# Attention and expert FFN on one core: the work behind the last head in a new order, three shared gates in banks y0, y1 and o, and the product for a pair's common tokens in high and low halves

## What is computed

```python
x = x + layernorm(attention(layernorm(x)))      # x: 8 x 512 x 256, 16 query heads, 4 key/value heads, D = 128, causal
x = x + layernorm(ffn(layernorm(x)))
# ffn, over the 4096 tokens:
scores = softmax(x @ gate_w.T)                  # 64 experts
topk_w, topk_idx = top_k(scores, 6)
# each expert takes the first CAP = 64 of the tokens that chose it:
d = (silu(buf @ w_gate) * (buf @ w_up)) @ w_down            # F = 176
y = sum of topk_w * d over a token's experts
y = y + (silu(x @ sh_gate.T) * (x @ sh_up.T)) @ sh_down.T   # shared expert, F_SH = 352
```

## Time and profile before

| what | us |
|---|---|
| median of 3 runs (1421.34 to 1427.04) | 1422.0 |
| the profiled execution | 1422.52 |
| its span in the trace | 1420.7 |
| the last output projection ends, the stage behind the heads begins | 1199.1 |
| first gather issued | 1241.56 |
| last scatter issued | 1374.23 |

### The profile page before, as it was taken

How to read it: one execution, slowest core, us unless ns; L and a number is a source line. 1 busy time by engine, 2 the same in 40 slices (tenths; PEclk the granted TensorE clock), 3 DMA queues, 4 the chain that set the end, 5 groups by cost and what they waited for, 6 DMA issues and landing times.

```text
span 1420.7 us, 27053 instructions
## 1 busy us (share of the span) xinstructions
PE 1331.6 (94%) x8963; PEld 1183.5 (83%) x8963; DVE 1098.7 (77%) x3655; ACT 843.2 (59%) x2315; POOL 799.9 (56%) x1052
## 2 busy tenths in 40 slices
PE   4999999999999999999999999999999998898950
PEld 3899999999999999999999999999999997854530
DVE  6777786889778977888788868896889788643438
ACT  5666666666666666666666666666666665443424
POOL 3666565556555655556455655565656554556644
PEclk9999999999999999999999999999999999898985
DMA  8100000100010001000100001000100017889986
GB/s 301 50 1 1 16 16 9 34 24 16 2 42 24 16 2 42 23 1 16 43 23 1 16 9 42 16 16 7 36 23 16 1 35 215 223 244 276 304 263 272
DMA packets 50235, 96.50 MB, mean 68 GB/s; under 512 B 4689, under 2 KB 36914, under 8 KB 50098
## 3 DMA queue, kind: packets, MB, share of 16 engines
q1 hardware_dynamic: 43954, 85.33, 18.5%
q0 software_dynamic: 6144, 9.44, 3.2%
HBM read 68.27 MB, written 26.49 MB: 67 GB/s over the span
## 4 chain that ended last, share of the span: by engine, by line
PE 86%; DVE 6%; POOL 3%; issue 2%; DMA 2%; ACT 1%; DVEq 0%; POOLq 0%; ACTq 0%
PE bank_s L623 19%; PE bank_t L623 19%; PE bank_o L623 17%; PE bank_y L623 12%; PE bank_f L623 8%; PE bank_t L708 4%; PE bank_s L708 4%; PE bank_f L708 2%; DMA ffn_sums<-dsum,idx_s 2%; POOL ffn_sums L1889 1%; DVE fstat L1679 1%; DVE fa L1674 1%; POOL xg L1876 1%; DVE fa L1699 1%; DVE pt_l L1352 0%
## 5 line engine op out<-in xcount | busy, mean ns | idle before, releaser
L1747 POOL TENSOR_TENSOR prob<-prob,rinv 128x512 f32<-128x512 f32 (+3 forms) x512 | 368.7, 726 | 320.8 <-DVE rinv L1346 309.9
L983 ACT ACTIVATE prob<-prob,negmax 128x512 f32<-128x512 f32 (+3 forms) x512 | 285.3, 557 | 85.1 <-DVE negmax L1333 76.8
L1734 POOL TENSOR_TENSOR q_l<-q_sum,q_h 128x128 fp32r<-128x128 f32 x254 | 182.5, 740 | 25.2 <-ACT q_h L963 25.2
L623 PE MATMUL bank_o<-pt_h,v_h 128*128 128x128 f32 (+3 forms) x512 | 180.0, 352 | 1.3 <-DVE pt_l L1352 1.3
L623 PE MATMUL bank_o<-pt_l,v_h 128*128 128x128 f32 (+3 forms) x512 | 165.1, 323 | 0.0
L623 PE MATMUL bank_o<-pt_h,v_l 128*128 128x128 f32 (+3 forms) x512 | 165.1, 322 | 0.0
L623 PE MATMUL bank_y<-wo_h,o_h 128*128 128x256 f32 x512 | 143.7, 281 | 3.2 <-DVE o_l L1358 2.8
L623 PE MATMUL bank_y<-wo_h,o_l 128*128 128x256 f32 x512 | 143.6, 280 | 0.0
L623 PE MATMUL bank_y<-wo_l,o_h 128*128 128x256 f32 x512 | 143.1, 279 | 0.0
L999 ACT ACTIVATE o_h<-bank_o,bkv_s 128x512 fp32r<-128x512 f32 x128 | 88.2, 689 | 78.1 <-PE bank_o L623 77.9
L992 ACT ACTIVATE pt_h<-bank_t 128x512 fp32r<-128x512 f32 (+3 forms) x208 | 89.1, 429 | 53.1 <-PE bank_o L623 50.9
(11 more groups left out here) (425 smaller groups left out, 4118.7 us busy)
## 6 DMA issues: line engine op xcount, KB each, us to landing
w_gu<-in_w_in SPq DMA_DIRECT2D x32, 704.0 KB
w_dn<-in_w_out SPq DMA_DIRECT2D x32, 320.0 KB
xio<-in_x SPq DMA_DIRECT2D x16, 512.0 KB, 4.3
token_table<-rows SPq DMA_DIRECT2D x8, 640.0 KB, 3.7
ffn_sums<-keys SPq DMA_DIRECT2D x4, 1024.0 KB
x_rows<-xio SPq DMA_DIRECT2D x8, 512.0 KB, 2.9
ffn_sums<-ytr SPq DMA_DIRECT2D x16, 256.0 KB, 2.1
fx<-x_rows SPq DMA_DIRECT2D x8, 512.0 KB
```

Source lines behind the costliest of these rows:

```text
L623: return pe.matmul(o, l, r, start=start, stop=stop, skip_group_check=True)
L983: act.activation(p_, p_, ACT.Exp, bias=negmax[:, r, i:i + 1], scale=-1.0, accum_out=rsum[:, r, i:i + 1]).then_inc(exp_made, 1)
L1734: pool.tensor_tensor(l_[:, cols], sum_of(step)[:, cols], plain(h_)[:, cols], ALU.subtract).then_inc(pos_low, 1)
L1747: pool.tensor_tensor(p_, p_, rinv[:, r, i:i + 1].to_broadcast([P, (i + 1) * P]), ALU.mult).then_inc(prob_made, 1)
```

## The change

Behind the heads:

- `LEFT`: three gate steps, (L1, 0, 0), (L1, 0, 1) and (LAST, 1, 0), use the banks y0, y1 and o instead of ring banks.
- `GATES`: the two steps that DVE does are now n = 2 of batch L1 (96 columns); n = 0 of it go over ACT and POOL.
- PE begins with four gates, puts halves of two gates between the transposes and the router products, turns each mask half at once, and makes `shared_down(L1, 1)` right behind. Each engine's order is written anew to fit.
- `shift` (a 128 x 4 product) moves from DVE to POOL; the softmax weights move from DVE to ACT (four activations with a scale), in one piece after one reciprocal; the second half's logits have a buffer of their own.
- POOL makes the first gate product between the two pairs of inverse roots, and begins the second only when DVE has finished the norm (`x2_normed`).
- SP stores the token rows before the weights of pairs 10 and 11; pair 11's are loaded behind `firsts_dram`.
- POOL's gathers wait for `gather_made`, which DVE sets behind the two casts to `idx_g`, not for `index_made`, three small instructions later.

In the experts' stage `add_second` has two float32r passes (`sec_h`, `sec_l`) for one float32 product: ACT makes `sec_h` with one more copy, DVE makes `sec_l` with one more subtraction (`second_rest`), which stands behind `half_w` of the pair after next.

```diff
-        GATES = ((L1, 1, 1), (L1, 1, 2), (L1, 0, 1), (L1, 0, 2), (LAST, 1, 0), (LAST, 1, 1), (LAST, 1, 2),
+        GATES = ((L1, 1, 0), (L1, 1, 1), (L1, 0, 0), (L1, 0, 1), (LAST, 1, 0), (LAST, 1, 1), (LAST, 1, 2),
                  (LAST, 0, 0), (LAST, 0, 1), (LAST, 0, 2))
+        LEFT = {step: Chan(bank[n], sem(f"{n}_gate_full"), sem(f"{n}_gate_taken"))
+                for step, n in ((("gu", L1, 0, 0), "y0"), (("gu", L1, 0, 1), "y1"), (("gu", LAST, 1, 0), "o"))}
...
-            for j in range(NWA, NW):
+            for j in range(NWA, NW - 2):
                 load_pair(j)
             store_rows(LAST)
-            store_ffn(LAST - 1, 1)
+            load_pair(NW - 2)
+            store_ffn(L1, 1)
             store_x2(LAST)
...
+            load_pair(NW - 1)
             sp.wait_ge(dma_firsts, 16)
...
             for n in range(NF):
-                gate_up(LAST - 1, 1, n)
-            gate_up(LAST - 1, 0, 0)
-
-            for step in (turn_x2, route):
-                for k in range(2):
-                    step(LAST, k)
-            gate_up(LAST - 1, 0, 1)
-            gate_up(LAST - 1, 0, 2)
-
+                gate_up(L1, 1, n)
+            gate_up(L1, 0, 2)
+
+            pe.wait_ge(var_made, VARS.index(("x2", LAST, 0)) + 1)
+            gate_up(L1, 0, 0, (0,))
+            turn_x2(LAST, 0)
+            gate_up(L1, 0, 0, (1,))
+            turn_x2(LAST, 1)
+            route(LAST, 0)
+            pe.wait_ge(var_made, VARS.index(("x2", LAST, 1)) + 1)
+            gate_up(L1, 0, 1, (0,))
+            route(LAST, 1)
+            gate_up(L1, 0, 1, (1,))
             turn_mask(LAST, 0)
-            gate_up(LAST, 1, 0, (0,))
+            gate_up(LAST, 1, 0)
             turn_mask(LAST, 1)
-            gate_up(LAST, 1, 0, (1,))
+
+            shared_down(L1, 1)
             gate_up(LAST, 1, 1)
-            shared_down(LAST - 1, 1)
             gate_up(LAST, 1, 2)
-            shared_down(LAST - 1, 0)
...
             def add_second(j):
 
                 pe.wait_ge(same_made, j + 1)
-                pe.wait_ge(second_made, j + 1)
-                mm(bank[f"t{j % 2}"][0:CAP, 0:E], same[j % 2][CAP:2 * CAP, :], dsum[j % ND][CAP:2 * CAP, :], stop=True
-                   ).then_inc(same_in, 1)
+                pe.wait_ge(second_low, j + 1)
+                to, at_ = bank[f"t{j % 2}"][0:CAP, 0:E], slice(CAP, 2 * CAP)
+                mm(to, same[j % 2][at_, :], sec_h[at_, :])
+                mm(to, same[j % 2][at_, :], sec_l[at_, :], stop=True).then_inc(same_in, 1)
...
                 act.wait_ge(down_in, j + 1)
-                act.activation(dsum[j % ND][CAP:2 * CAP, :], bank[f"t{j % 2}"][CAP:2 * CAP, 0:E], ACT.Copy
-                               ).then_inc(second_made, 1)
+                d_ = bank[f"t{j % 2}"][CAP:2 * CAP, 0:E]
+                act.activation(sec_h[CAP:2 * CAP, :], d_, ACT.Copy)
+                act.activation(dsum[j % ND][CAP:2 * CAP, :], d_, ACT.Copy).then_inc(second_high, 1)
...
+            def second_rest(j):
+                at_ = slice(CAP, 2 * CAP)
+                dve.wait_ge(second_high, j + 1)
+                dve.tensor_tensor(sec_l[at_, :], bank[f"t{j % 2}"][at_, 0:E], plain(sec_h[at_, :]), ALU.subtract
+                                  ).then_inc(second_low, 1)
...
+            pool.wait_ge(x2_normed, LAST + 2)
             gate_product(1)
...
-            pool.wait_ge(index_made, 1)
+            pool.wait_ge(gather_made, 1)
```

More of the change, by code:

```diff
@@ L207, in build @@
         second = place("second", [P, 3, NP], F32)
-        same = [place(f"same{i}", [P, CAP], F32) for i in range(2)]
+        same = [place(f"same{i}", [P, CAP], F32R) for i in range(2)]
         twice = [place(f"twice{i}", [P, 1], F32) for i in range(2)]
@@ L374, in use, with logit_of @@
             return c.bank, c.full, c.taken, u
+        VARS = [("x", 0)]
+        for b_ in range(NB):
+            if b_:
+                VARS.extend([("y", b_ - 1), ("x2", b_ - 1)])
+            if b_ < LAST:
+                VARS.append(("x", b_ + 1))
+        VARS.extend([(name, LAST, k) for name in ("y", "x2") for k in range(2)])
+        def logit_of(b, k):
+            return logit_b if (b, k) == (LAST, 1) else logit
         def x2_of(b, k):
@@ L1025, in route @@
                     c = 2 * k + i
-                    last = act.activation(rows[:, c, E:ROW], logit[:, i, 0:NE], ACT.Exp, bias=rmax[:, c:c + 1],
+                    last = act.activation(rows[:, c, E:ROW], logit_of(b, k)[:, i, 0:NE], ACT.Exp, bias=rmax[:, c:c + 1],
                                           accum_out=psum_[:, c:c + 1])
@@ L1137, in gate_in_high @@
                 act.activation(lanes[lane][0][0:fn, n, :], made[0:fn, :], ACT.Copy).then_inc(a_high[lane], 1)
-            gate_tanh_(L1, 1, 0)
             gate_out(0)
             gate_out(1)
-            gate_tanh_(L1, 0, 0)
+            gate_tanh_(L1, 1, 2)
+            gate_in_high(0)
+            gate_tanh_(L1, 0, 2)
             turn_x2(LAST, 0)
-            gate_high(L1, 1, 0)
             turn_x2(LAST, 1)
-            gate_in_high(0)
-            gate_high(L1, 0, 0)
             gate_in_high(1)
+            gate_high(L1, 1, 2)
+            gate_out(2)
             route(LAST, 0)
-            gate_out(2)
+            gate_out(3)
             route(LAST, 1)
-            gate_out(3)
             gate_in_high(2)
+            gate_out(4)
+            gate_in_high(3)
+            gate_high(L1, 0, 2)
+            act.wait_ge(sums_inverted, 1)
+            for c in range(TT):
+                last = act.activation(rows[:, c, E:ROW], rows[:, c, E:ROW], ACT.Copy, scale=pinv[:, c:c + 1])
+            last.then_inc(weights_made, 2)
+            gate_out(5)
             act.wait_ge(shift_made, 1)
@@ L1168, in scalar_program @@
             gate_out(7)
+            shared_down(L1, 0)
             gate_in_high(6)
@@ L1248, in variance @@
                 last.then_inc(var_made, 1)
-            VARS = [("x", 0)]
-            for b_ in range(NB):
-                if b_:
-                    VARS.extend([("y", b_ - 1), ("x2", b_ - 1)])
-                if b_ < LAST:
-                    VARS.append(("x", b_ + 1))
-            VARS.extend([(name, LAST, k) for name in ("y", "x2") for k in range(2)])
             def normed(o, s_, i):
@@ L1389, in route @@
                 done(dve.tensor_copy(left[:, :, 0:NE], halves[:, :, 1, :]))
-                dve.tensor_tensor(logit[:, :, 0:NE], halves[:, :, 0, :], left[:, :, 0:NE], ALU.add).then_inc(taken, 1)
+                dve.tensor_tensor(logits[:, :, 0:NE], halves[:, :, 0, :], left[:, :, 0:NE], ALU.add).then_inc(taken, 1)
                 dve.wait_ge(taken, u + 1)
                 for i in range(2):
-                    last = dve.max(top8[:, i, :], logit[:, i, :])
+                    last = dve.max(top8[:, i, :], logits[:, i, :])
                 done(last)
@@ L1397, in route @@
                 for i in range(2):
-                    last = dve.match_replace(left[:, i, :], top8[:, i, :], logit[:, i, :], -BIG)
+                    last = dve.match_replace(left[:, i, :], top8[:, i, :], logits[:, i, :], -BIG)
                 done(last)
@@ L1583, in vector_program @@
                     step(LAST, k)
+            dve.wait_ge(router_exp, 2 * LAST + 2)
+            dve.reciprocal(pinv[:], psum_[:]).then_inc(sums_inverted, 1)
             for r in range(CAP // 8):
@@ L1619, in vector_program @@
                 at_ = slice(u * CAP, (u + 1) * CAP)
-                dve.tensor_copy(idx_g[at_, :], turned[at_, 0, :, u])
+                last = dve.tensor_copy(idx_g[at_, :], turned[at_, 0, :, u])
+            last.then_inc(gather_made, 1)
             dve.tensor_copy(idx_s[0:CAP, :], turned[0:CAP, 1, :, 0])
@@ L1649, in expert_act @@
                 last.then_inc(half_made, 1)
+                if j > 1:
+                    second_rest(j - 2)
                 dve.wait_ge(half_made, j + 1)
@@ L1670, in vector_program @@
                 targets(j)
+            second_rest(NP - 2)
+            second_rest(NP - 1)
             def add_sums(b):
```

74 lines of the change are left out of this document (43 added, 31 removed).

## The result

The changed kernel takes 1418.95 us (median of 15 runs, 1416.31 to 1420.56) against 1423.40 us for the kernel before in the same series (15 runs, 1421.34 to 1427.60). The ratio is 0.9971, with a 95% interval of 0.9960 to 0.9981: a gain of 4.5 us, 0.3%, less than the 0.5% that the prediction calls measurable. Forecast were 1412.3 us and a range up to 1418.5. The profiled execution took 1418.23 us with a span of 1416.4, against 1422.5 and 1420.7.

A forecast was written before the change was run, and what follows sets the result against it. Late POOL and PE, not the picks, were taken to bound the first gather, and DMA the experts' stage: 1422.5 - 10.5 (earlier gather) + 0.8 (gathers meeting loads) - 0.5 (cheaper add_second) = 1412.3 us, range 1406.5 to 1418.5.

The forecast's parts named there:

- picks at 1214.55 (1214.6): DVE behind the heads: shorter waits and moved work let the picks start at 1214.6, 4.1 us earlier.
- POOL done at 1229.74 (1229.3): POOL behind the heads: with waits for ACT cut to 2.0 us, done at 1229.3, 10.3 earlier.
- the forecast gain of 10.2: Whole kernel: from 1422.5 us to 1412.3 us.
- tables at 1228.4: DVE behind the picks: tables done at 1228.4, or 1230.5 if three small steps each wait for POOL.
- 0.3 for DVE steps beside POOL: Before the first gather: allowance of 0.3 us for small DVE steps waiting on POOL, giving 1231.0.
- 1228.5 as forecast: PE before the tables: its last shared_down product, waiting for POOL's low half, ends at 1228.5.
- I charge 0.8 for the first (0 to 3): First gather: meeting pair 11's weights and firsts in flight costs 0.8 us, from 0 to 3.
- - 0.5 (the halves): Experts' stage: of 7.8 us from the cheaper add_second on PE, only 0.5 counted, for the last rounds.
- the distance from first gather to last scatter of 132 us: Experts' stage: distance stays at 132 us; a change beyond 3 us either way means the prediction is wrong.
- that the whole gain reaches the end rests on this: Experts' stage: first weight reload follows the first pair's output, so the saturated DMA stretch begins 10 us earlier.
- part is given back: Rival: clock drop, ACT starving POOL, gathers colliding with pair 11, or scatter stalls leave 4 to 7 us, 1417; chance 0.24.
- Slower: Rival, experts' rounds: ACT's copy and DVE's subtraction delay add_second, losing 0.57 us a round, 1430; chance 0.04.

The follow-up runs named there:

- tables_alone: Changed kernel, but POOL starts its last gate product only when DVE's tables are done: 1415.82 us (one run).
- pair11_late: Changed kernel with pair 11's weights loaded behind the last two stores of the feed-forward sums, not ahead of the gathers: 1417.51 us, ratio 0.9930.
- light versions: Kernel before and changed kernel, both without the second expert's gate and up weights in pairs 12 to 31: 1411.49 us (0.9905) and 1404.63 us (0.9855).
- order_only: Changed kernel with the old float32 product for the common tokens, so only the new order behind the heads: 1417.89 us, ratio 0.9937.
- order_pair11: Changed kernel with the old float32 product and pair 11's weights loaded behind the last two stores of the sums: 1414.96 us, ratio 0.9929.
- series 3: Two by two on one chip: changed kernel with halves or float32 product, pair 11's weights ahead of gathers or behind the stores: 1415.92 to 1418.63 us.
- halves_only: Kernel before with only the common tokens' product changed, to high and low halves: 1426.98 us, ratio 1.0002.
- halves_but_last_p11: Changed kernel with the float32 product in the last six pairs and pair 11's weights behind the last stores: 1414.56 us, ratio 0.9920.
- best_float: Changed kernel with the float32 product for all pairs and pair 11's weights behind the last stores: 1416.89 us, ratio 0.9939.
- (light): Changed kernel with halves against the same with float32 product, both without some weight loads in pairs 12 to 31: 1402.02 against 1404.55 us.
- the first four series: The first four of five groups of follow-up runs, each version's ratio taken to the kernel before on the same chip.
- f_order: Changed kernel with the old float32 product, pair 11's weights still ahead of the gathers: 1417.36 us, ratio 0.9933.
- after_again: Changed kernel measured again, unchanged: 1419.86 us, ratio 0.9962.

## Why the prediction was wrong

Behind the heads the working held nearly to the letter: picks at 1214.55 (1214.6), the norm's second half at 0.73 instead of 1.52, no clock drop in front of the tables, POOL done at 1229.74 (1229.3). The error is in four terms, and they add up to the 5.9 us between the forecast gain of 10.2 and the 4.3 of the profiled executions.

- **"tables at 1228.4"**, with "0.3 for DVE steps beside POOL": 1230.26. I wrote down that the small steps could wait for POOL, with 2.1 us and an end at 1230.5, and put 0.3 into the sum. Four of the six steps took 0.6 to 0.8 us each, against 0.18 to 0.34 for all six in tables_alone. That agrees with the rule of the Trainium skill that the prediction cites, page SBUF — State Buffer, section "SBUF: two separate sides", that whoever starts first holds the shared ports for its whole instruction. PE's product in front of the tables ended at 1229.3 and not at 1228.5 as forecast, and PE then stood 0.99 us for the tables. The two delays together cost 1.6 us, 1.0 of it by the tables; 0.3 were in the sum, and 1.3 of 10.5 went: the first gather came at 1232.3 for 1231.0.
- **"I charge 0.8 for the first (0 to 3)"**: 1.8. The mechanism was right, only the size was off by 1.0. pair11_late, back at 8.2 us from gather to activation, shows that the load of pair 11 was all of it.
- **"- 0.5 (the halves)"**, and with it "the distance from first gather to last scatter of 132 us": the distance became 136.8, beyond the 3 us that I had named as the sign of an error. Of the 4.1 us more, 1.8 are the gather's landing, 0.3 net lie between the first activation and the last reload, and 2.1 behind the last reload. Of these 2.1 only the last pair's part is shown: with the new order and the float32 product the same stretch was 32.2 to 34.2 us in five profiles with all loads, against 32.3 before and 34.4 here. Shown is that the halves lengthen the last pair's chain by 1.1 to 2.2 us, which my sum did not contain: I priced ACT's copy and DVE's subtraction as hidden behind PE's `w_gu` products, and behind the last pair there are none. The -0.5 "for the last rounds" is not borne out: there the chain got longer. In the middle the bound was the DMA as I had decided, which the light versions show. This part is 2.8 us off (0.5 + 0.3 + 2.1, less 0.1 of rounding).
- **The end**: 0.8 us more from last scatter to end, not in my sum. In the changed kernel SP asks for the first sums at 1369.31, while the last scatter has only begun at 1369.15, and the second copy's sums are asked for at 1374.88, 5.7 us behind it; before it was 3.8 us (1374.23 to 1378.00). The runs don't bear out that these reads are in the last scatter's way: order_only and order_pair11 asked for both copies as late as the kernel before (2.0 and 3.8 us behind the last scatter) and took 47.4 and 47.8 us from it to the end, where the changed kernel took 47.2 and the kernel before 46.5. Over all 20 profiles this stretch is 46.2 to 47.8 us, so the cause of the 0.8 stays open and it may be chance.

The sentence "that the whole gain reaches the end rests on this: ... begins 10 us earlier" thus failed at its premise: the first reload came 6.9 us earlier, since the late landing and then the low clock (the 16 products of 4.80 us for 3.97) stood before it. From there to the last reload the lead passed through whole (7.2). The rival "part is given back" is what happened, by its collision with pair 11 and a tail that it did not name. "Slower" did see the piece on ACT and DVE, 0.57 us a round in blocked rounds; there the distance from the first scatter to the last reload is 85.3 against 85.4, so it was not paid.

**What stays open** is what the halves are worth in all. Pairs on one chip point both ways: +1.1 and +2.7 us (series 3), +0.4 (halves_only to the kernel before), -2.3 (halves_but_last_p11 to best_float, all pairs but six), -2.5 (light); in each of the five the ranges overlap. The intervals between scatters differ from profile to profile of one kernel by more than that: the stretch behind the last reload was 32.5 to 34.8 us in three profiles of the changed kernel. I can't separate a gain of 0 to 2 us in the middle from this. Nor is it settled how much of the changed kernel's 0.9971 to 0.9944 is the chip.

## What to carry to other kernels

A start that comes earlier is worth what it is worth at the first instruction of the next stage, so price what is in flight at the new moment: a load that did no harm when the gather came 10 us later took 1.8 of 9.2 us here, and in each of the first four series the complete version with the lowest median had it behind the gathers. A product made cheaper on one engine by work on two others gave nothing measurable here, where transfers hold the rounds, and lengthened the last pair's chain, where nothing hides it; try the old form for the last few. When more buffers only move a wait from one engine to the next, stop adding them and look at what lands late.

## What the runs showed of the hardware

- VectorE's small steps between tiles in SBUF took 0.6 to 0.8 us beside GpSimd's products and 0.18 to 0.34 beside none. In the changed kernel the long steps end as GpSimd's instructions do (`tok` at 1227.60 and 1228.42 beside ends at 1227.56 and 1228.37, `sct` at 1229.88 beside 1229.74).
- The granted clock fell at the end of the experts' stage with either product, but earlier in some executions with halves: in the 3.5 us behind the last turn it was 0.68 in the changed kernel and 1.00 in f_order. The last down product took 1.6 to 2.0 us in five of ten profiles with halves to the last pair, and 1.09 in all ten without. What decides between the five and the other five is open: in after_again TensorE waited as long for `sec_l` and the clock fell only behind the product.
- Taking 7.0 MB of some 35 out of the stage shortened a scatter's median landing from 7.4 to 5.4 us and the kernel by 13.7 us, though in the kernel before no engine's waits in that stage name the weights.
